# A node MLP run between edge groups: x added on VectorE, second product one chunk later

## The chip, the cores and the metric

The kernel runs on one NeuronCore of a Trainium2 chip. The metric is the device time of one execution in microseconds (us); lower is better. Three runs of the kernel before gave 4202.96 to 4210.07 us.

## What is computed

Two graph layers over 6,250 nodes and 200,000 edges, edges sorted by destination. The change touches the first:

```python
e = edge_attr @ W_edge + b_edge
msg = jax.nn.relu(x[src] + e)
agg = jax.ops.segment_sum(msg, dst, num_segments=x.shape[0])
h = (1.0 + eps) * x + agg
h = jax.nn.relu(h @ W1 + b1) @ W2 + b2
mean = jnp.mean(h, axis=0)
var = jnp.var(h, axis=0)
h = (h - mean) * jax.lax.rsqrt(var + BN_EPS) * gamma + beta
return jax.nn.relu(h)
```

A layer norm of x + h follows, then an attention layer and another layer norm. Everything is float32.

## The kernel before

**Groups.** Layer 0 walks over 196 groups of 1,024 edges. GpSimd (POOL) fetches a group's source rows with 8 indirect DMAs of 128 rows (`gather`, L377) into one of 4 slots of `rows`. TensorE (PE) multiplies the group's edge features in two halves (`edge_products`, L854, after a bias product L851) into banks 0 and 1 (half 0) or 2 and 3 (half 1). VectorE (DVE) adds each half into the rows (`add_edges`, L972), ScalarE (ACT) applies Relu (L952), and PE sums the messages into a window of 128 nodes with one-hot matrices (`sum_half`, L865), ACT copies the window (L956), PE transposes it (`turn_window`, L874) and DVE adds it into `acc` (`add_window`, L986). PE's body for group g holds the transposition of g-3, the second half of the sums of g-2, the first half of the products of g, the first half of the sums of g-1, and the second half of the products of g.

**What ties the engines.** POOL may start the gathers of group g when PE has finished the first products of group g-2:

```python
pool.wait_ge(half_done, 2 * (g - RING) + 5)
```

PE in its turn needs DVE's adds of the group before (`added`), and DVE needs the gathered rows (`rows_in`).

**Chunks.** The nodes are split into 14 chunks of 448. Since the edges are sorted, a chunk's sums are complete long before the last group. `rounds` runs four groups at a time and calls `finish_nodes(c, at)` on each engine after the round in which chunk c is complete (`at` is that round's last group). In this run 13 chunks (0 to 12) are finished in this way between rounds, 24 and 16 groups apart at first, 12 and 8 later and 4 between the last two; the last chunk (13) is finished after all groups by `last_nodes`. I call the 13 places boundaries.

**A boundary before.** PE makes three products of four matmuls each: x by (1+eps)W1 (`w1x`, L896) and the sums in `acc` by W1 (L901), which accumulate in banks 0 and 1; then, after ACT's Relu (L436), the second product by W2 (L909) into banks 2 and 3. Each matmul of 448 columns shows as two records, so a product is 8. PE then waits for ACT's copy with bias into `node_x` (L440) and only then goes on with the next group. DVE takes the statistics (`bn_stats`, L450) of the chunk before. SyncE (SP) loads x of a chunk into `x_in[0]` when PE has consumed the chunk before (`load_nodes`, L820). The end of layer 0 is the same three products for chunk 13, statistics, batch norm.

Of the kernel before, what the change touches and what calls it, by code (L numbers as in the profile page):

```python
# [22 lines left out]
ALU = mybir.AluOpType  # L23
# [6 lines left out]
P = 128  # L30
# [39 lines left out]
def build(nc, t):  # L70
    with ExitStack() as ctx:
# [3 lines left out]
        def sem(name):  # L75
            return ctx.enter_context(nc.semaphore(name))
# [179 lines left out]

        layer0, layer1 = Layer(0), Layer(1)
        half_done, added, bias_ready = sem("half_done"), sem("added"), sem("bias_ready")

        def two(name):  # L260
            return [sem(f"{name}{b}_") for b in range(2)]
# [555 lines left out]

        def single0_loads(sp):
            def load_nodes(c, at):
                sp.wait_ge(a_pe1, HALF * c)  # L820
                sp.sem_inc(passed, 1)
                sp.dma_start(x_in[0], t["x_t"][:, :, bass.ds(c * CHUNK, CHUNK)]).then_inc(a_in, 16)

            def body(i, u, g):
                if first_round(i):
                    return
                sp.wait_ge(layer0.rows_in[u], 16 * J * i)
                sp.dma_start(idx[:, u, :], t["src_idx"][g]).then_inc(layer0.idx_in[u], 16)
# [14 lines left out]
        def single0_matmuls(pe):  # L843
# [42 lines left out]
                    sum_half((u - 1) % RING, g - 1, 0, n < 3)  # L886
                edge_products(i, u, g, 1).then_inc(half_done, 1)

            def finish_nodes(c, at):
                pe.wait_ge(w1x_ready, 1)  # L890
                pe.wait_ge(a_in, 16 * c + 16)
                pe.wait_ge(a_act2, c)
                pe.wait_ge(added, 2 * at + 1)
                for m in range(HALF):
                    for k in range(HALF):
                        pe.matmul(banks[m][:, 0:CHUNK], w1x[:, k, m * P:(m + 1) * P], x_in[0][:, k, :],  # L896
                                  start=(k == 0), stop=False)
# [13 lines left out]
                last.then_inc(a_pe2, 1)  # L911
                pe.wait_ge(a_act2, c + 1)

            def finish_last(c, at):
                pe.wait_ge(w1x_ready, 1)
                pe.wait_ge(a_in, 16 * c + 16)
                pe.wait_ge(a_act2, c)
                for m in range(HALF):
                    for k in range(HALF):
                        pe.matmul(banks[m][:, 0:CHUNK], w1x[:, k, m * P:(m + 1) * P], x_in[0][:, k, :],  # L920
                                  start=(k == 0), stop=False)
                pe.wait_ge(layer0.group_done, GROUPS)
                for m in range(HALF):
                    for k in range(HALF):
                        last = pe.matmul(banks[m][:, 0:CHUNK], w1[:, k, m * P:(m + 1) * P],
                                         acc[:, k, bass.ds(c * CHUNK, CHUNK)], start=False, stop=(k == HALF - 1))
                    last.then_inc(a_pe1, 1)
                for m in range(HALF):
                    for k in range(HALF):
                        if m == 0:  # L930
                            pe.wait_ge(a_act1, 2 * c + k + 1)
                        last = pe.matmul(banks[2 + m][:, 0:CHUNK], w2[:, k, m * P:(m + 1) * P], x_in[1][:, k, :],
                                         start=(k == 0), stop=(k == HALF - 1))
                last.then_inc(a_pe2, 1)
# [13 lines left out]
        def single0_act(act):  # L948
            def relu(u, g, b):
                act.wait_ge(added, 2 * g + b + 1)  # L950
                half = rows[:, u, 4 * b:4 * b + 4, 0:D]
                act.activation(half, half, ACT.Relu).then_inc(layer0.msg_ready, 1)  # L952

            def copy_window(u, g, halves):
                act.wait_ge(half_done, halves)
                act.copy(agg_sb[:, 0:D], banks[4 + u % 2][:, 0:D]).then_inc(layer0.agg_copied, 1)  # L956

            def body(i, u, g):
                relu(u, g, 0)
# [3 lines left out]
            c0 = rounds(act, body, mlp_act(act, 0, 2))  # L963
            copy_window((GROUPS - 2) % RING, GROUPS - 2, 2 * GROUPS + 1)
            copy_window((GROUPS - 1) % RING, GROUPS - 1, 2 * GROUPS + 3)
            last_nodes(act, mlp_act(act, 0, 2), c0)

        def single0_vector(dve):
            def add_edges(i, u, g, b):
                dve.wait_ge(half_done, 2 * g + b + 1)  # L970
                half = rows[:, u, 4 * b:4 * b + 4, 0:D]
                dve.tensor_tensor(half, half, psum[:, 2 * b:2 * b + 2, :].rearrange("p b (j d) -> p (b j) d", j=2),  # L972
                                  ALU.add).then_inc(added, 1)

            def make_onehot(u, g):
                for j in range(J):
                    last = dve.tensor_scalar(onehot[:, u % 2, j, :], iota[:, :],  # L977
                                             dst_off[:, bass.ds(g, 1), j:j + 1].rearrange("p g j -> p (g j)"), None,
                                             ALU.is_equal)
                last.then_inc(layer0.onehot_ready, 1)  # L980

            def add_window(u, g, halves):
                base = dve.value_load(plan[0:1, 0, bass.ds(g, 1)], min_val=0, max_val=NODES)
                at = bass.ds(base, WIN)
                dve.wait_ge(half_done, halves)
                dve.tensor_tensor(acc[:, :, at], acc[:, :, at],  # L986
                                  banks[6 + u % 2][:, 0:HALF * WIN].rearrange("p (k n) -> p k n", k=HALF), ALU.add)
                dve.drain().then_inc(layer0.group_done, 1)

            def body(i, u, g):  # L990
                dve.wait_ge(layer0.rows_in[u], 16 * J * (i + 1))
# [5 lines left out]
            c0 = rounds(dve, body, mlp_dve(dve, 1))  # L997
# [185 lines left out]
        def _(pe):  # L1183
# [7 lines left out]
                single0_matmuls(pe)  # L1191
            with pe.Else():
                pass_matmuls(pe, layer0, 0)
            pe.wait_ge(a_act2, CHUNKS)

            def mean_over(x, out, done):
                for k in range(HALF):
# [49 lines left out]
        def _(act):  # L1247
# [6 lines left out]
                single0_act(act)  # L1254
            with act.Else():
                pass_act(act, layer0, 0)
            act.wait_ge(bn_var, 1)
            act.activation(bn_tmp[:, :], mv[:, :, 1], ACT.Sqrt, bias=bn_eps[:, :]).then_inc(bn_sqrt, 1)
            act.wait_ge(bn_ready, 1)
# [343 lines left out]
```

## Time and profile before

| | |
|---|---|
| median of three runs | 4208.57 us (4202.96 to 4210.07) |
| the profiled execution's own time | 4207.65 us |
| its span, first to last instruction | 4205.7 us |
| layer 0 (first gather to the last Relu'd node product) | about 3 to 2066 us of the span |
| mean granted TensorE clock | 0.879 |
| busy share over the span: PE, PE weight loads, DVE, ACT, POOL | 75%, 57%, 55%, 19%, 73% |

Times in rows are microseconds from the start of the span. PE is TensorE, PEld its weight loads, POOL GpSimd, SPq or ACTq an engine's queue. Brackets at the end of a timeline row give the engine's idle time before it and what released it. A granted clock of 1.00 is 2.4 GHz and 0.50 is 1.2 GHz.

### The profile page before, as it was taken

To read this page: it belongs to the slowest core of one execution; us is meant where nothing else is said; L and a number is where in the kernel's file an instruction comes from. 1 tells how busy PE (TensorE), PEld (TensorE's weight loads), DVE (VectorE), ACT (ScalarE), POOL (GpSimd) and SP (SyncE) were. 2 spreads that over 40 slices of the span, in tenths; PEclk is the share of its full clock that TensorE was granted. 3 is DMA by queue.
4 is the path that set the end of the run, shared out by engine and by line. 5 is a ranking of instruction groups with operands and counts; after the bars stand their busy time and mean duration, and the time that the engine had idled before them with its cause. 6 is when DMAs were issued, how large, how long until landed. Compare 5 with 4: busy or idle time off the path is not lost.

```text
span 4205.7 us, 55810 instructions
## 1 busy us (share of the span) xinstructions
PE 3147.9 (75%) x13605; PEld 2400.0 (57%) x13705; DVE 2322.7 (55%) x5665; ACT 798.6 (19%) x1490; POOL 3064.9 (73%) x3229
## 2 busy tenths in 40 slices
PE   7888788898888888889876666666666666666666
PEld 5666666676666666767554444444444444444544
DVE  5444444344444443434476666666666666766676
ACT  2222222222222222222240000010110111111112
POOL 7777777777777777767347777777777777777775
PEclk9999999999999999999897777877878778788777
DMA  5555555455545454545245555555555555555554
GB/s 186 154 157 155 155 158 157 151 158 153 154 149 166 152 153 148 168 140 163 74 128 157 160 157 156 161 160 160 162 156 165 161 161 164 160 165 161 160 169 122
DMA packets 321499, 651.40 MB, mean 155 GB/s; under 512 B 149711, under 2 KB 170425, under 8 KB 321465
## 3 DMA queue, kind: packets, MB, share of 16 engines
q0 software_dynamic: 150528, 414.45, 34.3%
q1 hardware_dynamic: 164448, 230.16, 17.5%
q10 hardware_dynamic: 6489, 6.40, 0.5%
q8 instruction: 12, 0.20, 0.0%
q14 instruction: 22, 0.18, 0.0%
HBM read 637.67 MB, written 13.08 MB: 155 GB/s over the span
## 4 chain that ended last, share of the span: by engine, by line
POOL 30%; PE 23%; issue 18%; DMA 12%; DVEq 7%; DVE 6%; ACT 2%; ACTq 1%; POOLq 1%; SPq 0%
POOL rows L377 30%; PE psum L865 7%; PE psum L854 7%; DMA rows<-z_tab,idx 6%; DMA rows<-in_x,idx 5%; DVEq L731 4%; DVE rows L972 2%; PE psum L851 1%; PE psum L584 1%; PE psum L874 1%; DVEq L727 1%; PE psum L909 1%; PE psum L896 1%; PE psum L1217 1%; PE psum L901 1%
## 5 line engine op out<-in xcount | busy, mean ns | idle before, releaser
L377 POOL DMA_INDIRECT rows<-in_x,idx x1568 | 1510.2, 963 | 531.8 <-issue 450.0
L377 POOL DMA_INDIRECT rows<-z_tab,idx x1568 | 1503.6, 959 | 482.5 <-issue 455.5
L972 DVE TENSOR_TENSOR rows<-rows,psum 128x1024 f32<-128x1024 f32 x392 | 478.5, 1221 | 1153.7 <-DMA rows<-in_x,idx 803.3
L584 PE MATMUL psum<-rows,onehot 128*128 128x260 f32 x3136 | 1059.5, 511 | 23.6 <-issue 23.3
L584 PEld LDWEIGHTS psum<-rows,onehot 128*128 128x128 f32 x3136 | 805.8, 263 | 208.8 <-issue 32.0
L854 PE MATMUL psum<-weights,edge_room 128*128 128x256 f32 x3136 | 816.7, 384 | 6.3 <-issue 1.5
L865 PE MATMUL psum<-rows,onehot 128*128 128x256 f32 x3136 | 776.9, 393 | 0.0
L854 PEld LDWEIGHTS psum<-weights,edge_room 128*128 128x128 f32 x3136 | 607.3, 194 | 161.1 <-issue 8.2
L952 ACT ACTIVATE rows<-rows 128x1024 f32<-128x1024 f32 x392 | 414.3, 1057 | 1491.7 <-DVE rows L972 1491.6
L865 PEld LDWEIGHTS psum<-rows,onehot 128*128 128x128 f32 x3136 | 602.3, 197 | 78.1
L801 DVE TENSOR_TENSOR rows<-rows,psum 128x1024 f32<-128x1024 f32 x392 | 460.7, 1216 | 77.9 <-ACT psum L673 77.9
L578 PE MATMUL psum<-ed_win,hot_t 128*128 128x12 bf16 x1576 | 72.6, 172 | 447.0 <-DVE hot_t L722 447.0
L670 ACT ACTIVATE rows<-expo 128x32 f32<-128x32 f32 x196 | 44.9, 229 | 1574.8 <-DVE expo L705 1567.1
L578 PEld LDWEIGHTS psum<-ed_win,hot_t 128*128 128x128 bf16 x1576 | 55.3, 101 | 503.7 <-DVE hot_t L722 252.2
L977 DVE TENSOR_SCALAR onehot<-iota,dst_off 128x128 f32<-128x128 f32 x1568 | 328.1, 296 | 0.0
L758 DVE TENSOR_TENSOR onehot<-dst_off,psum 128x1024 f32<-128x1024 f32 x196 | 239.3, 1221 | 85.1 <-issue 84.8
L398 PE MATMUL psum<-ident,agg_sb 128*128 128x128 f32 x392 | 82.0, 292 | 260.3 <-ACT agg_sb L639 260.3
L874 PE MATMUL psum<-ident,agg_sb 128*128 128x128 f32 x392 | 84.1, 297 | 250.6 <-ACT agg_sb L956 202.3
L851 PE MATMUL psum<-onehot 128*128 128x512 bf16 x685 | 264.1, 386 | 9.0 <-DVEq L1383 7.0
L697 DVE TENSOR_TENSOR score<-score,rows 128x32 f32<-128x32 f32 x196 | 38.1, 194 | 388.0 <-DMA rows<-z_tab,idx 382.9
L722 DVE TENSOR_SCALAR hot_t<-dst_t,node_at 128x256 bf16<-128x256 int32 x788 | 236.8, 362 | 0.1
L398 PEld LDWEIGHTS psum<-ident,agg_sb 128*128 128x128 f32 x392 | 39.9, 142 | 334.6 <-issue 334.6
(152 smaller groups left out, 1787.6 us busy)
## 6 DMA issues: line engine op xcount, KB each, us to landing
dst_t<-in_dst_jp SPq DMA_DIRECT2D x197, 512.0 KB
edge_room<-in_edge_t SPq DMA_DIRECT2D x196, 512.0 KB, 3.9
rows<-in_x,idx POOLq DMA_INDIRECT x1568
rows<-z_tab,idx POOLq DMA_INDIRECT x1568
dst_t<-in_x_t SPq DMA_DIRECT2D x28, 448.0 KB, 5.3
z_tab<-edge_room SPq DMA_DIRECT2D x14, 455.0 KB, 3.5
idx<-in_src_idx SPq DMA_DIRECT2D x392, 4.0 KB, 1.6
out<-onehot ACTq DMA_DIRECT2D x13, 448.0 KB, 3.4
```

The costliest lines, as they stand in the source:

```text
L377: nc.gpsimd.indirect_dma_start(rows[:, u, j, 0:width], None, table, bass.IndirectOffsetOnAxis(ap=idx[:, u, j:j + 1], axis=0)).then_inc(L.r ...
L584: last = pe.matmul(agg_ps[0:WIN, 0:width], onehot[:, hot, j, :], rows[:, u, j, 0:width], start=(j == 0), stop=(j == J - 1))
L722: last = dve.tensor_scalar(hot_t[:, part], dst_t[:, u % 2, part], node_at[:, bass.ds(g, 1)], None, ALU.is_equal)
L731: dve.drain().then_inc(L.group_done, 1)
L758: dve.tensor_tensor(onehot[:, hot, :, :], off.unsqueeze(2).to_broadcast([P, J, WIN]), iota_ps.unsqueeze(1).to_broadcast([P, J, WIN]), ALU. ...
L801: dve.tensor_tensor(z, z, w.unsqueeze(3).to_broadcast([P, J // 2, HEADS, HEAD_D]), ALU.mult).then_inc(L.msg_ready, 1)
L851: pe.matmul(bank[:, 0:2 * D], ones_bf[:, :], bias_rhs[:, :], start=True, stop=False)
L854: last = pe.matmul(bank[:, h * D:(h + 1) * D], edge_in[:, u, j * P:(j + 1) * P], w_edge[:, :], start=False, stop=(h == 1))
L865: last = pe.matmul(banks[4 + u % 2][:, 0:D], onehot[:, u % 2, j, :], rows[:, u, j, 0:D], start=(j == 0), stop=(j == J - 1))
L952: act.activation(half, half, ACT.Relu).then_inc(layer0.msg_ready, 1)
L972: dve.tensor_tensor(half, half, psum[:, 2 * b:2 * b + 2, :].rearrange("p b (j d) -> p (b j) d", j=2), ALU.add).then_inc(added, 1)
L977: last = dve.tensor_scalar(onehot[:, u % 2, j, :], iota[:, :], dst_off[:, bass.ds(g, 1), j:j + 1].rearrange("p g j -> p (g j)"), None, ALU ...
```

## The change

DVE adds (1+eps)x into `acc` for the chunk (one `scalar_tensor_tensor` over 128x896), counted by a new semaphore `a_sum`. PE's first product is then one product of `acc` by W1, into banks 2 and 3. The second product of chunk c is made at the boundary of chunk c+1, into banks 0 and 1, before the first product of chunk c+1; that of chunk 12 is made after the loop over all groups. ACT does its bias of chunk c-1 before the Relu of chunk c. DVE's statistics come two chunks later at a boundary, and those of the chunks left over stand ahead of the last `add_window`. SP's load of x waits for DVE's addition and no longer for PE. PE and ACT wait for the constants at the start. At the end of a boundary PE waits for both Relus of chunk c. `w1x` is still made, and no longer used in this path.

```diff
         def single0_loads(sp):
             def load_nodes(c, at):
-                sp.wait_ge(a_pe1, HALF * c)
+                sp.wait_ge(a_sum, c)
...
-            def finish_nodes(c, at):
-                pe.wait_ge(w1x_ready, 1)
-                pe.wait_ge(a_in, 16 * c + 16)
-                pe.wait_ge(a_act2, c)
-                pe.wait_ge(added, 2 * at + 1)
+            def first_product(c):
+                pe.wait_ge(a_sum, c + 1)
                 for m in range(HALF):
                     for k in range(HALF):
-                        pe.matmul(banks[m][:, 0:CHUNK], w1x[:, k, m * P:(m + 1) * P], x_in[0][:, k, :],
-                                  start=(k == 0), stop=False)
-                pe.wait_ge(layer0.group_done, at + 1 - LAG)
+                        last = pe.matmul(banks[2 + m][:, 0:CHUNK], w1[:, k, m * P:(m + 1) * P],
+                                         acc[:, k, bass.ds(c * CHUNK, CHUNK)], start=(k == 0), stop=(k == HALF - 1))
+                    last.then_inc(a_pe1, 1)
+
+            def second_product(c):
+                pe.wait_ge(a_act1, 2 * c + 2)
                 for m in range(HALF):
                     for k in range(HALF):
-                        last = pe.matmul(banks[m][:, 0:CHUNK], w1[:, k, m * P:(m + 1) * P],
-                                         acc[:, k, bass.ds(c * CHUNK, CHUNK)], start=False, stop=(k == HALF - 1))
-                    last.then_inc(a_pe1, 1)
-                pe.wait_ge(added, 2 * at + 2)
-                for m in range(HALF):
-                    for k in range(HALF):
-                        if m == 0:
-                            pe.wait_ge(a_act1, 2 * c + k + 1)
-                        last = pe.matmul(banks[2 + m][:, 0:CHUNK], w2[:, k, m * P:(m + 1) * P], x_in[1][:, k, :],
+                        last = pe.matmul(banks[m][:, 0:CHUNK], w2[:, k, m * P:(m + 1) * P], x_in[1][:, k, :],
                                          start=(k == 0), stop=(k == HALF - 1))
                 last.then_inc(a_pe2, 1)
+
+            def finish_nodes(c, at):
+                pe.wait_ge(added, 2 * at + 1)
+                with pe.If(c > 0):
+                    second_product(c - 1)
+                pe.wait_ge(added, 2 * at + 2)
+                first_product(c)
                 pe.wait_ge(a_act2, c + 1)
+                pe.wait_ge(a_act1, 2 * c + 2)
 
             def finish_last(c, at):
...
+                first_product(c)
+                pe.wait_ge(a_act2, c + 1)
+                second_product(c)
 
             pe.wait_ge(bias_ready, 1)
+            pe.wait_ge(const_in, 16 * WEIGHT_LOADS)
             c0 = rounds(pe, body, finish_nodes)
+            pe.wait_ge(added, 2 * GROUPS - 1)
+            with pe.If(c0 > 0):
+                second_product(c0 - 1)
...
+            def first_relu(c):
+                for k in range(HALF):
+                    act.wait_ge(a_pe1, 2 * c + k + 1)
+                    act.activation(x_in[1][:, k, :], banks[2 + k][:, 0:CHUNK], ACT.Relu,
+                                   bias=cols[:, 0, k:k + 1]).then_inc(a_act1, 1)
...
+            def finish_nodes(c, at):
+                with act.If(c > 0):
+                    act.reg_mov(before, c - 1)
+                    second_bias(act.snap(before, min_val=0, max_val=CHUNKS - 2))
+                first_relu(c)
...
+            def add_nodes(c):
+                chunk = acc[:, :, bass.ds(c * CHUNK, CHUNK)]
+                dve.wait_ge(a_in, 16 * c + 16)
+                dve.scalar_tensor_tensor(chunk, x_in[0], eps1[:, 0:1], chunk, ALU.mult, ALU.add).then_inc(a_sum, 1)
...
+            def finish_nodes(c, at):
+                add_nodes(c)
+                earlier_statistics(c, 2)
...
             add_window((GROUPS - 2) % RING, GROUPS - 2, 2 * GROUPS + 3)
+            earlier_statistics(c0, 2)
+            earlier_statistics(c0, 1)
             add_window((GROUPS - 1) % RING, GROUPS - 1, 2 * GROUPS + 4)
-            last_nodes(dve, mlp_dve(dve, 2), c0)
+            last_nodes(dve, finish_last, c0)
```

## Rows read from the trace of the kernel before

**Rows 1.** Groups of instructions, whole span: line, engine, operation, count, busy and mean ns
```profile
L377 POOL DMA_INDIRECT rows<-in_x,idx x1568 | 1510.2, 963 | 531.8 <-issue 450.0 <-PE psum L854 80.9 <-DMA idx<-in_src_idx 1.0
...
L436 ACT ACTIVATE dst_t<-psum,cols 128x448 f32<-128x448 f32 x28 | 17.7, 633 | 25.8 <-PE psum L901 19.7 <-PE psum L925 6.1
...
L1428 DVE TENSOR_TENSOR rows<-rows,edge_room 128x896 f32<-128x896 f32 x14 | 15.3, 1092 | 2.4 <-issue 0.5
```

**Rows 2.** Waits of POOL, 43 to 2045 us: total us, times, longest
```profile
POOL rows L377 <- issue: 440.8, 1409, 1.9
POOL rows L377 <- PE psum L854: 80.9, 128, 7.0
```

**Rows 3.** Timeline of POOL: gathers that start late, all behind boundaries
```profile
593.73 0.95 POOL L377 DMA_INDIRECT rows<-in_x,idx  x1 [1.67 <-PE psum L854]
...
841.23 0.95 POOL L377 DMA_INDIRECT rows<-in_x,idx  x1 [4.42 <-PE psum L854]
...
1006.28 0.95 POOL L377 DMA_INDIRECT rows<-in_x,idx  x1 [3.19 <-PE psum L854]
1009.10 0.96 POOL L377 DMA_INDIRECT rows<-in_x,idx  x1 [1.87 <-issue]
...
1679.07 0.95 POOL L377 DMA_INDIRECT rows<-in_x,idx  x1 [2.22 <-PE psum L854]
...
1974.96 0.95 POOL L377 DMA_INDIRECT rows<-in_x,idx  x1 [3.20 <-PE psum L854]
...
2022.23 0.95 POOL L377 DMA_INDIRECT rows<-in_x,idx  x1 [7.03 <-PE psum L854]
```

**Rows 4.** Chain in order of time at the third boundary: start, us, what
```profile
984.85 1.23 DVE rows L972
...
986.12 3.27 PE psum L896 x8
...
992.40 3.26 PE psum L909 x8
...
997.04 2.33 issue
999.37 0.59 PE psum L874 x2
```

**Rows 5.** Timeline of DVE at the same boundary
```profile
988.24 1.22 DVE L972 TENSOR_TENSOR rows<-rows,psum 128x1024 f32<-128x1024 f32 x1 [0.19 <-issue]
```

**Rows 6.** Windows behind two boundaries: last three numbers clock, DMA, GB/s
```profile
999.40:1006.30 6.90, 6.90 (x26) 5.63 (x27) 0.89 (x1) 0.00 (x0) 2.88 (x4) 0.75 0.26 76
588.50:593.70 5.20, 5.20 (x25) 4.45 (x26) 0.84 (x1) 0.00 (x0) 2.87 (x3) 1.00 0.34 101
```

**Rows 7.** Timeline of PE, last two boundaries
```profile
1968.05 0.44 PE L874 MATMUL psum<-ident,agg_sb 128*128 128x128 f32 x2 [3.72 <-issue]
...
2001.75 3.17 PE L896 MATMUL psum<-dst_t,w1x 128*128 128x448 f32 x8
...
2014.03 0.68 PE L874 MATMUL psum<-ident,agg_sb 128*128 128x128 f32 x2 [2.85 <-issue]
```

**Rows 8.** Timeline of the end of layer 0
```profile
2055.65 3.24 PE L920 MATMUL psum<-dst_t,w1x 128*128 128x448 f32 x8
2056.19 0.42 DVE L986 TENSOR_TENSOR acc<-acc,psum 128x256 f32 x1 [0.83 <-PE psum L874]
...
2058.73 3.17 PE L925 MATMUL psum<-acc,weights 128*128 128x448 f32 x8
```

**Rows 9.** Timeline of DVE and POOL near the start
```profile
17.14 1.79 DVE L1343 TENSOR_TENSOR dst_off<-node_x,first_f 128x1568 f32<-128x1568 int32 x1
...
18.07 1.69 POOL L377 DMA_INDIRECT rows<-in_x,idx  x1 [0.30 <-issue]
```

**Rows 10.** Timeline of DVE, start
```profile
25.76 5.39 DVE L1384 MEMSET acc<- 128x6400 f32 x1 [1.48 <-DMA hot_t<-in_att_dst]
...
32.36 1.22 DVE L972 TENSOR_TENSOR rows<-rows,psum 128x1024 f32<-128x1024 f32 x1 [0.62 <-PE psum L854]
```

More of the change, by code:

```diff
@@ L258, in build @@
         half_done, added, bias_ready = sem("half_done"), sem("added"), sem("bias_ready")
+        a_sum = sem("a_sum")
         def two(name):
@@ L910, in finish_nodes @@
                                          start=(k == 0), stop=(k == HALF - 1))
                 last.then_inc(a_pe2, 1)
+            def finish_nodes(c, at):
[4 more added lines that the diff above has]
+                first_product(c)
                 pe.wait_ge(a_act2, c + 1)
+                pe.wait_ge(a_act1, 2 * c + 2)
             def finish_last(c, at):
-                pe.wait_ge(w1x_ready, 1)
@@ L916, in finish_last @@
[L916 to L934, printed above, removed]
+                first_product(c)
+                pe.wait_ge(a_act2, c + 1)
+                second_product(c)
@@ L962, in body, with second_bias, finish_last @@
                 relu(u, g, 1)
-            c0 = rounds(act, body, mlp_act(act, 0, 2))
+            def first_relu(c):
[3 more added lines that the diff above has]
+                                   bias=cols[:, 0, k:k + 1]).then_inc(a_act1, 1)
+            before = act.alloc_register("chunk_before")
+            def second_bias(c):
+                act.wait_ge(a_pe2, c + 1)
+                for k in range(HALF):
+                    ins = act.activation(node_x[:, k, bass.ds(c * CHUNK, CHUNK)], banks[k][:, 0:CHUNK],
+                                         ACT.Identity, bias=cols[:, 1, k:k + 1])
+                ins.then_inc(a_act2, 1)
+            def finish_nodes(c, at):
[3 more added lines that the diff above has]
+                first_relu(c)
+            def finish_last(c, at):
+                first_relu(c)
+                second_bias(c)
+            act.wait_ge(const_in, 16 * WEIGHT_LOADS)
+            act.sem_inc(a_act2, 1)
+            c0 = rounds(act, body, finish_nodes)
+            with act.If(c0 > 0):
+                act.reg_mov(before, c0 - 1)
+                second_bias(act.snap(before, min_val=0, max_val=CHUNKS - 2))
             copy_window((GROUPS - 2) % RING, GROUPS - 2, 2 * GROUPS + 1)
             copy_window((GROUPS - 1) % RING, GROUPS - 1, 2 * GROUPS + 3)
-            last_nodes(act, mlp_act(act, 0, 2), c0)
+            last_nodes(act, finish_last, c0)
         def single0_vector(dve):
@@ L996, in body, with statistics, earlier_statistics, finish_last @@
                 add_edges(i, u, g, 1)
-            c0 = rounds(dve, body, mlp_dve(dve, 1))
+            prev = dve.alloc_register("prev_chunk_single")
+            def add_nodes(c):
+                chunk = acc[:, :, bass.ds(c * CHUNK, CHUNK)]
+                dve.wait_ge(a_in, 16 * c + 16)
+                dve.scalar_tensor_tensor(chunk, x_in[0], eps1[:, 0:1], chunk, ALU.mult, ALU.add).then_inc(a_sum, 1)
+            def statistics(c, n):
+                for k in range(HALF):
+                    dve.bn_stats(stats[:, k, bass.ds(c, 1), :].rearrange("p a s -> p (a s)"),
+                                 node_x[:, k, bass.ds(c * CHUNK, n)])
+            def earlier_statistics(c, back):
+                with dve.If(c > back - 1):
+                    dve.wait_ge(a_act2, c + 2 - back)
+                    dve.sem_inc(passed, 1)
+                    dve.reg_mov(prev, c - back)
+                    statistics(dve.snap(prev, min_val=0, max_val=CHUNKS - 2), CHUNK)
+            def finish_nodes(c, at):
+                add_nodes(c)
+                earlier_statistics(c, 2)
+            def finish_last(c, at):
+                add_nodes(c)
+                dve.wait_ge(a_act2, c + 2)
+                statistics(c, TAIL if isinstance(c, int) else CHUNK)
+            c0 = rounds(dve, body, finish_nodes)
             add_window((GROUPS - 3) % RING, GROUPS - 3, 2 * GROUPS + 1)
             add_window((GROUPS - 2) % RING, GROUPS - 2, 2 * GROUPS + 3)
+            earlier_statistics(c0, 2)
+            earlier_statistics(c0, 1)
             add_window((GROUPS - 1) % RING, GROUPS - 1, 2 * GROUPS + 4)
-            last_nodes(dve, mlp_dve(dve, 2), c0)
+            last_nodes(dve, finish_last, c0)
         def nodes(i, b):
@@ L1193, in _ @@
                 pass_matmuls(pe, layer0, 0)
-            pe.wait_ge(a_act2, CHUNKS)
+            pe.wait_ge(a_act2, CHUNKS + 1)
             def mean_over(x, out, done):
@@ L1256, in _ @@
                 pass_act(act, layer0, 0)
+                act.sem_inc(a_act2, 1)
             act.wait_ge(bn_var, 1)
```

## The prediction

> **What bounds the kernel now.** I read the groups of instructions first. POOL's gathers are the largest: 0.96 us each, and with the 0.30 us that normally lies between two (the bracket of the gather in [rows 9]) a group of eight takes 10.1 us [rows 1]. The change touches layer 0 alone, so the question is when POOL does not keep that pace there. The waits of POOL say it: 128 times the gather came behind a product of PE, 80.9 us in all [rows 2]. At 0.30 us each, 38.4 of these are its ordinary gap; 42.5 are real. The timeline of POOL shows where: one late gather behind each of the 13 boundaries, 1.4 us over the ordinary gap at the first, about 2.9 at six, about 4 at three (the row at 841 us stands for them), 1.9 at one, 2.9 at the twelfth, 6.7 at the last [rows 3]; 0.6 of the 42.5 lies at the start, before any boundary. Behind seven of them the second gather is late too, by 1.57 us, as at 1009.10 [rows 3]. What POOL loses to boundaries is therefore 41.9 + 7 x 1.57 = 52.9 us. That is the stake. Between boundaries PE waits for rows, and what PE does there costs nothing.
>
> The chain in order of time at one boundary gives the mechanism [rows 4]. Call the start of DVE's addition of half 0 of the last group t0 (984.85). PE starts the x product at t0+1.27, three products follow one another, two ACT copies end at 997.04, and then come 2.33 us that no wait explains: PE's loop turn and its reads of the next limits. PE resumes at t0+14.52. The late gather started at 1006.28, 2.89 us late [rows 3], so POOL was ready at 1003.39, t0+18.54, and from resuming to that gather PE needed 6.91 us. With the clock at 1.00 that stretch is 5.2 us; here it had 0.75 on average [rows 6].
>
> **Removed from PE's path.** The x product is gone, and the second product moves ahead of the first, where it needs nothing that is new. I lay the new boundary out in the same frame.
>
> - PE: second product of c-1 from t0+1.27. The branch before it is not in the trace; below it cannot be under 0, above I take the whole 2.33 us of the loop turn [rows 4], and I use 0.3, since the loop turn holds several branches and loads. It ends at 1.27+0.3+3.26 = t0+4.85.
> - DVE: its addition of half 1 starts at 988.24, t0+3.39, takes 1.22 us [rows 5], and the next instruction starts about 0.06 before its end, at t0+4.55. The new addition over 128x896 is priced by the 1.09 us of the tensor-tensor of that size with both inputs in SBUF [rows 1]; a form with one more operand may cost up to 1.3. I take 1.1: sums ready at t0+5.65. This, and not the second product, releases PE, so 0.8 us of branch are covered.
> - PE: first product, from a standing start 3.27 us [rows 4]: t0+8.92. ACT's second Relu, 0.63 us and some 0.1 for two semaphores [rows 1]: t0+9.65. The loop turn 2.33: PE resumes at t0+12.0, 2.5 us earlier than before.
> - ACT: its bias of c-1 (two copies, 1.2 us) falls after its Relu of half 1, between t0+5.7 and t0+7; the first Relu is ready for it only at t0+7.4. Covered, and late by 0.7 us if the second product comes 1.5 us late.
> - DVE's statistics, SP's load of x and the constants: the statistics stand where DVE waits for PE afterwards. The load waits for t0+5.65 of the boundary before instead of the end of PE's second of three products; it is a whole boundary early. The constants have landed when DVE's memset starts at 25.76, while DVE's first addition starts only at 32.36 behind other work [rows 10]; PE's start slips by at most 1.5 us under that. All nothing.
>
> **The clock.** The idle time before PE resumes was 3.72 us at the boundary before the last and 2.85 at the last [rows 7]; it becomes 12.0-8.9 = 3.1. At the last one the clock fell all the same, and at the first, after a longer idle time, it stayed at 1.00 [rows 6]. I count on no gain here and leave the stretch of 6.91 us (5.2 to 8.2) as each boundary had it.
>
> **What remains of the eleven boundaries before 1954 us.** They cost 41.9-2.9-6.7 = 32.3 in first gathers and six times 1.57 = 9.4 in second ones: 41.7. With PE 2.5 earlier the three of about 4 keep 1.6, 1.2 and 1.6 = 4.4; the six of 2.9 keep 0.4; the two short ones nothing.
>
> **What the new addition does to POOL.** DVE's instruction with two SBUF inputs ran from 17.14 to 18.93; the gather that started in it at 18.07 took 1.69 us instead of 0.96 [rows 9]: it was held 0.73, that is the 0.86 that DVE still had, less 0.13. At our boundary the gathers start every 1.26 us back from 1003.39, one of them at 989.5, t0+4.65, just inside the new addition (4.55 to 5.65): held by about 0.87. Other boundaries lie a little differently (nothing to 1.0); I take 0.75. POOL is the bound, so this counts, except where it waits for PE anyway. So eight boundaries lose 0.75 each (6.0, the 0.4 is inside) and three lose 4.4: 10.4. The eleven give back 41.7-10.4 = 31.3 us.
>
> A page of the Trainium skill, SBUF — State Buffer, section Who interferes with whom, says that a VectorE instruction with two SBUF inputs contends only with GpSimd reads, and infers that a tensor-tensor does not stall descriptor generation. By that inference the hold would be 0, the eleven would lose 6.8 and the sum below would be 3.6 us better; [rows 9] speak against it.
>
> **The last two boundaries and the end.** From 1968.05 on PE is the bound: it goes through four groups and reaches the last boundary at 2001.75 without idle time [rows 7]. There the order before took 12.28 us. New: 0.3 + 3.0 (second product, back to back) + 3.27 + 0.73 for the Relu + 1.5 loop turn (the 2.85 of idle time less ACT's last copies) = 8.8, 3.5 less. With the 2.5 of the twelfth boundary PE is 6.0 us earlier. After the groups it has one second product more, 3.26+0.3, on its path. For chunk 13 the x product started at 2055.65 and the next at 2058.73 [rows 8]. New: the last addition into `acc` ends at 2056.6, the new addition at 2057.8, the first product at 2061.1, and the second starts after both Relus at 2061.8, where it was 2061.9. So the end costs 3.4. The three together give 6.0-3.4 = 2.6 us.
>
> **Sum.** 31.3+2.6 = 33.9 us from the profiled execution's 4207.65: 4173.7. The median of the runs is 0.9 higher: **4174.5 us**.
>
> **Rivals.**
> - *Nothing is held and the clock stays up* (more gain). For it: the first boundary kept 1.00 [rows 6], and the new idle time is shorter than at eleven of them. All 41.7 come back, plus 6.0-3.4, plus up to 2.8 twice for clock on PE's last stretch: 44 to 50 us, 4158 to 4164; the missing hold alone gives 4171, inside my own case. Chance 0.17. The inference of the Trainium skill's page SBUF — State Buffer, named above, is the first half of it.
> - *POOL still stalls* (less gain). The branch costs 2.33 and the new addition 1.3: PE resumes 1.5 to 1.7 later than I laid out, first gathers gain only about 0.9 each, the second gathers stay late: eleven boundaries give some 11 us, the end nothing: 8 to 20 us, 4188 to 4200. Against it: each branch inside the 2.33 can only be a part of it. Chance 0.14.
> - *Slower.* One mechanism: the new conditional blocks make PE's queue fetch code out of order on entering and on leaving, 2.33 us each, 4.7 in all. 0.8 is covered, so PE resumes 3.9-2.5 = 1.4 later than before, 13 x 1.4 = 18 us and 2 at the end: 4228. It decides from 3.4 us per boundary on. For it is only that 2.33 us of the loop turn are unexplained. Chance 0.05. The Trainium skill, Runtime: NRT & Kernel Launch, section Instruction fetch mechanics, says that a taken branch to code outside the fetched pages stalls for a fetch; no row here shows one at a boundary by itself.
> - *The change moves nothing*: POOL's late gathers have another cause than PE's return, say the transfers. Against it, their size follows PE's: 5.2 us after resuming with the clock at 1.00, 6.9 with it at 0.75 [rows 6]. Chance 0.03.
>
> **Chances and range.** My case, 26 to 42 us of gain, has 0.61. Within 0.2% (8.4 us, about what a measurement of this kernel can tell from no change) I put 0.03, above it 0.05, below 0.92. The likeliest case alone is 4166 to 4183. The range of 8 in 10 takes in most of the first rival and the upper part of the second: 4158 to 4191.
>
> **What would show it.** The three products at a boundary become two, with the second first; the span from t0 to PE's next transposition is 12.0 instead of 14.5. POOL's waits behind L854 fall from 80.9 towards 45, the 1.87 rows go mostly; one gather of 1.7 us stands beside each new addition. The first transposition after a boundary has about 3.1 us of idle time before it. Between boundaries a group still takes 10.1 us, and layer 1 is unchanged. The prediction is wrong if PE's resume moves by less than 1 us (branch), if the gathers at boundaries are held for more than 1 us, or if POOL's late gathers keep their size while PE comes earlier.

## The result and the profile after

The changed kernel takes 4180.19 us (median of 4 runs, 4174.65 to 4182.70) beside 4205.76 us (4 runs, 4200.05 to 4210.07): 0.9936 of the time before, 95% interval 0.9921 to 0.9952, 25.6 us less. Two more samples, each beside its own runs of the kernel before, gave 0.9932 (0.9920 to 0.9944) and 0.9934 (0.9921 to 0.9948). The profiled execution took 4182.70 us with a span of 4180.9, 24.8 less than the span of before.

The groups of instructions, whole span (columns as in [rows 1]):

```profile
L378 POOL DMA_INDIRECT rows<-in_x,idx x1568 | 1522.9, 971 | 484.9 <-issue 448.6 <-PE psum L855 35.3 <-DMA idx<-in_src_idx 1.0
...
L1020 DVE SCALAR_TENSOR_TENSOR acc<-dst_t,eps,acc 128x896 f32 (+1 forms) x14 | 16.0, 1146 | 0.3 <-issue 0.3
```

POOL's idle time before the gathers of layer 0 fell from 531.8 to 484.9, and its busy time rose from 1510.2 to 1522.9 [rows 1]: the change gives and takes on the same engine. The addition takes 1.15 us. The waits of POOL, 43 to 2110 us:

```profile
POOL rows L378 <- issue: 439.5, 1428, 1.9
POOL rows L378 <- PE psum L855: 35.3, 109, 1.5
```

Beyond the ordinary 0.30 us, these waits for PE come to 35.3 - 109 x 0.30 = 2.6 us, where they were 42.5 [rows 2]. Some late gathers now stand under "issue" as well. All gathers that start late behind a boundary, added up gather by gather, lose 5.9 us, where they lost 52.9. The chain at the third boundary says how, start, length, what; t0 is 983.79 here:

```profile
988.24 1.16 DVE acc L1020
989.40 0.24 issue
989.63 3.28 PE psum L894 x8
992.91 0.02 issue
992.94 0.64 ACT dst_t L954
993.58 2.37 issue
995.96 0.68 PE psum L875 x2
```

DVE's addition starts at t0+4.45 and releases PE's first product; one Relu and the loop turn follow, and PE resumes at t0+12.17; before it was 14.52 [rows 4]. The timeline of the same stretch, DVE, POOL and PE:

```profile
983.79 1.22 DVE L990 TENSOR_TENSOR rows<-rows,psum 128x1024 f32<-128x1024 f32 x1 [5.52 <-DMA rows<-in_x,idx]
...
984.70 0.96 POOL L378 DMA_INDIRECT rows<-in_x,idx  x1 [0.30 <-issue]
...
985.30 3.27 PE L902 MATMUL psum<-dst_t,weights 128*128 128x448 f32 x8 [0.72 <-DVE rows L990]
...
988.24 1.14 DVE L1020 SCALAR_TENSOR_TENSOR acc<-dst_t,eps,acc 128x896 f32 x1
...
988.59 1.63 POOL L378 DMA_INDIRECT rows<-in_x,idx  x1 [0.30 <-issue]
...
989.30 1.15 DVE L1024 BATCH_NORM_STATS2 stats<-node_x  x2
989.32 1.14 ACT L962 ACTIVATE node_x<-psum,cols 128x448 f32 x2
...
995.96 0.68 PE L875 MATMUL psum<-ident,agg_sb 128*128 128x128 f32 x2 [3.05 <-issue]
996.43 3.62 PE L866 MATMUL psum<-rows,onehot 128*128 128x256 f32 x8
...
1004.10 0.95 POOL L378 DMA_INDIRECT rows<-in_x,idx  x1 [1.25 <-PE psum L855]
...
1006.92 0.95 POOL L378 DMA_INDIRECT rows<-in_x,idx  x1 [1.87 <-issue]
```

The deferred second product runs from t0+1.5 to t0+4.8, in the time in which PE would wait for DVE. The gather that starts inside the addition takes 1.63 us; the one at 984.70, which starts inside DVE's addition into `rows` (one input in SBUF, one in PSUM), takes 0.96. The late gather is 0.95 us late, not 2.89 [rows 3], and the second one still 1.57; here the clock fell after the boundary (3.62 us for eight records instead of 1.89).

The end of layer 0, timeline:

```profile
2023.75 0.44 PE L875 MATMUL psum<-ident,agg_sb 128*128 128x128 f32 x2 [0.46 <-ACT agg_sb L944]
2024.50 2.21 DVE L1024 BATCH_NORM_STATS2 stats<-node_x  x4 [0.66 <-issue]
2026.62 0.40 DVE L1004 TENSOR_TENSOR acc<-acc,psum 128x256 f32 x1
2027.36 1.15 DVE L1020 SCALAR_TENSOR_TENSOR acc<-dst_t,eps,acc 128x896 f32<-128x896 f32 x1 [0.33 <-issue]
2028.56 5.33 PE L894 MATMUL psum<-acc,weights 128*128 128x448 f32 x8 [4.38 <-DVE acc L1020]
```

Before, the last transposition started at 2055.27 and the last addition into `acc` 0.9 us later, at 2056.19 [rows 8]. Here the addition stands behind four statistics and comes 2.9 us after the transposition's start, and PE then runs the first product with the clock down, 5.33 us for eight records. From the start of the last gather to the end of the last bias copy it is 30.5 us; before it was 23.5. Up to the last transposition it is 2.6 us more, behind it 4.3.

How far the profiled execution is ahead of the one before, place by place:

| place | before | after | ahead |
|---|---|---|---|
| t0 of the first boundary | 573.70 | 575.44 | -1.7 |
| t0 of the twelfth | 1953.52 | 1929.63 | 23.9 |
| PE resumes after the last | 2014.03 | 1982.48 | 31.6 |
| last gather starts | 2042.81 | 2008.66 | 34.2 |
| last bias copy ends | 2066.34 | 2039.15 | 27.2 |
| span | 4205.7 | 4180.9 | 24.8 |

### The profile page after: what moved, and what is told of

It is laid out like the page before. It is cut to its first block, busy times and chain, and to the rows that moved or that the text cites. A ratio compares the mean times of both kernels' runs of the same rounds, so it can differ in the third digit from the quotient of the medians.

```text
span 4180.9 us, 55635 instructions
## 1 busy us (share of the span) xinstructions
PE 3078.4 (74%) x13493; PEld 2355.7 (56%) x13593; DVE 2339.0 (56%) x5679; ACT 797.3 (19%) x1490; POOL 3078.8 (74%) x3229
## 3 DMA queue, kind: packets, MB, share of 16 engines
q1 hardware_dynamic: 164448, 230.16, 17.8%
## 4 chain that ended last, share of the span: by engine, by line
POOL 31%; PE 19%; issue 19%; DMA 12%; DVEq 8%; DVE 7%; ACT 2%; ACTq 1%; POOLq 1%; SPq 0%
POOL rows L378 31%; DMA rows<-z_tab,idx 7%; PE psum L866 6%; PE psum L855 6%; DMA rows<-in_x,idx 5%; DVEq L732 5%; DVE rows L990 2%; DVEq L728 1%; PE psum L852 1%; PE psum L474 1%; PE psum L1265 1%; PE psum L875 1%; PE psum L1246 1%; PE psum L894 1%; DVE rows L802 1%
## 5 line engine op out<-in xcount | busy, mean ns | idle before, releaser
L378 POOL DMA_INDIRECT rows<-in_x,idx x1568 | 1522.9, 971 | 484.9 <-issue 448.6
L585 PE MATMUL psum<-rows,onehot 128*128 128x260 f32 x3136 | 1024.8, 498 | 23.7 <-issue 23.6
L585 PEld LDWEIGHTS psum<-rows,onehot 128*128 128x128 f32 x3136 | 781.5, 255 | 198.4 <-issue 32.0
L866 PEld LDWEIGHTS psum<-rows,onehot 128*128 128x128 f32 x3136 | 600.4, 197 | 78.2
L995 DVE TENSOR_SCALAR onehot<-iota,dst_off 128x128 f32<-128x128 f32 x1568 | 329.9, 298 | 0.0
```

Of the source, the lines that this page charges most:

```text
L378: nc.gpsimd.indirect_dma_start(rows[:, u, j, 0:width], None, table, bass.IndirectOffsetOnAxis(ap=idx[:, u, j:j + 1], axis=0)).then_inc(L.r ...
L585: last = pe.matmul(agg_ps[0:WIN, 0:width], onehot[:, hot, j, :], rows[:, u, j, 0:width], start=(j == 0), stop=(j == J - 1))
L866: last = pe.matmul(banks[4 + u % 2][:, 0:D], onehot[:, u % 2, j, :], rows[:, u, j, 0:D], start=(j == 0), stop=(j == J - 1))
```

## The experiments

The times are medians of 5 to 12 runs; each ratio is to the kernel before in the same job. PE's return is the median over the boundaries of its profile, measured from t0.

| kernel | us | ratio (95%) | PE resumes | last gather to last bias copy |
|---|---|---|---|---|
| changed, 2nd sample | 4177.59 | 0.9932 (0.9920 to 0.9944) | t0+12.2 | 30.2 |
| addition only | 4251.10 | 1.0111 (1.0097 to 1.0124) | 17.8 | 23.2 |
| deferral only | 4197.80 | 0.9977 (0.9969 to 0.9986) | 14.0 | 27.4 |
| one SBUF input | 4175.98 | 0.9928 (0.9916 to 0.9940) | 12.2 | 30.8 |
| addition, wait filled | 4226.12 | 1.0048 (1.0035 to 1.0062) | 16.0 | 24.8 |
| late statistics | 4182.03 | 0.9936 (0.9922 to 0.9949) | 12.2 | 25.8 |
| split addition | 4176.52 | 0.9931 (0.9918 to 0.9945) | 11.7 | 30.0 |
| split, late statistics | 4175.44 | 0.9926 (0.9912 to 0.9939) | 11.7 | 26.4 |
| changed, 3rd sample | 4181.84 | 0.9934 (0.9921 to 0.9948) | 12.2 | 30.5 |
| split, late statistics, 2nd | 4174.24 | 0.9917 (0.9904 to 0.9931) | 11.7 | 27.9 |
| and second product moved | 4169.30 | 0.9910 (0.9896 to 0.9923) | 11.7 | 24.2 |
| the same, addition whole | 4173.49 | 0.9916 (0.9902 to 0.9929) | 12.2 | 24.2 |

**The changed kernel again**, unedited, in two jobs.

> The changed kernel once more, as the measure for the other runs on this chip. Both theories: 24 to 27 us under the kernel before, PE resumes 12.2 us after DVE's first addition of the boundary (t0), 12 gathers of 1.6 to 1.9 us, two to five late gathers behind the first boundaries.

> The changed kernel once more, on the chip of the next three, since differences of 2 to 10 us are at stake: 24 to 29 us under the kernel before.

Measured 30.1 and 26.5 us under the kernel before, the first more than expected. PE's return was the same in all three profiles; the late gathers varied (5.9, 9.2 and 11.2 us in all), and so did the number of boundaries behind which the clock fell: 4, 7 and 8 of 13. In the profile of the kernel before it fell behind 11.

**The addition alone.** Against the kernel before:

```diff
                 pe.wait_ge(a_act2, c)
                 pe.wait_ge(added, 2 * at + 1)
-                for m in range(HALF):
-                    for k in range(HALF):
-                        pe.matmul(banks[m][:, 0:CHUNK], w1x[:, k, m * P:(m + 1) * P], x_in[0][:, k, :],
-                                  start=(k == 0), stop=False)
-                pe.wait_ge(layer0.group_done, at + 1 - LAG)
+                pe.wait_ge(a_sum, c + 1)
                 for m in range(HALF):
...
-            c0 = rounds(dve, body, mlp_dve(dve, 1))
+            c0 = rounds(dve, body, added_first(mlp_dve(dve, 1)))
```

`added_first` puts `add_nodes(c)` of the changed kernel ahead of DVE's statistics; the second product stays in banks 2 and 3.

> One part alone: DVE adds (1+eps)x and PE's first product has four matmuls, but the second product stays at its own chunk and the statistics where they were. My theory: the gain needs both parts. The sums are ready at t0+5.65, first product to 8.9, second product to 12.2, ACT's two copies to 13.6, PE's loop turn to t0+16.0, that is 1.5 us later than the kernel before (14.5), because PE stands idle while DVE works. POOL's late gathers grow by 1.5 us each and 12 gathers are held: 15 to 25 us slower than the kernel before. The rival, that the gain is the 3.0 us of matmuls saved per boundary, expects about the gain of the whole change or more, 25 to 38 us faster than before.

Measured 43.4 us slower: the direction right, the size twice what I expected. POOL's late gathers come to 81.4 us instead of 52.9, and 12 gathers are held, 8.9 us in all. Timeline of PE and ACT at a boundary with t0 at 1124.64:

```profile
1130.49 4.74 PE L896 MATMUL psum<-acc,weights 128*128 x8 [5.05 <-DVE acc L990]
1133.76 0.63 ACT L437 ACTIVATE dst_t<-psum,cols 128x448 f32<-128x448 f32 x1 [3.49 <-PE psum L896]
1135.06 3.41 PE L904 MATMUL psum<-dst_t,weights 128*128 128x448 f32 x8
```

PE waited 5.05 us for DVE and then took 4.74 us for a product that takes 3.27 elsewhere: the clock fell inside it (1.00 from 1124.6 to 1130, 0.79 on average from 1130 to 1138). PE resumed at t0+17.6 here. The same product took 4.7 to 6.3 us at 12 of the 13 boundaries. Four matmuls fewer, and slower, because the work taken away had been lying under DVE's additions.

**The deferral alone.** Against the changed kernel:

```diff
-            def first_product(c):
-                pe.wait_ge(a_sum, c + 1)
+            def first_product(c, done):
+                pe.wait_ge(w1x_ready, 1)
+                pe.wait_ge(a_in, 16 * c + 16)
+                for m in range(HALF):
+                    for k in range(HALF):
+                        pe.matmul(banks[2 + m][:, 0:CHUNK], w1x[:, k, m * P:(m + 1) * P], x_in[0][:, k, :],
+                                  start=(k == 0), stop=False)
+                pe.wait_ge(layer0.group_done, done)
                 for m in range(HALF):
...
-                add_nodes(c)
                 earlier_statistics(c, 2)
```

> The other part alone: the x product stays on PE (w1x), the second product of a chunk comes at the next boundary, DVE adds nothing; the statistics are two chunks late as in the change. My theory: second product to t0+4.9, x product to 7.9, product of the sums to 10.9, Relu and loop turn to t0+13.9, 0.6 us earlier than the kernel before and 1.8 later than the change; no gather is held; the late gathers stay at 2 us each, less 1.7 where the clock no longer falls. At the end of layer 0 some 5 us more than before. In all 5 to 20 us faster than before, so less than the change. A rival, that the deferral is the whole gain and the addition on DVE adds nothing, expects 25 us or more, as in the change.

Measured 9.9 us faster than the kernel before, as expected. The chain at the boundary with t0 at 1235.82:

```profile
1235.82 1.23 DVE rows L995
1237.05 0.27 issue
1237.32 3.27 PE psum L907 x8
1240.59 3.17 PE psum L894 x8
1243.77 3.02 PE psum L899 x8
1246.79 0.02 issue
1246.81 0.64 ACT dst_t L959
1247.45 2.37 issue
1249.83 0.43 PE psum L874 x2
```

Three products in a row, only one Relu and the loop turn behind them: t0+14.0, as worked out. No gather is held, POOL's late gathers sum to 34.2 us. So the parts do not add: +43 and -10 apart, -30 together in the same job.

**One SBUF input.** The output lacks (1+eps)x.

```diff
-    dve.scalar_tensor_tensor(chunk, x_in[0], eps1[:, 0:1], chunk, ALU.mult, ALU.add).then_inc(a_sum, 1)
+    dve.bn_stats(onehot[:, 2, 3, 0:6], acc[:, 0, bass.ds(c * CHUNK, CHUNK)])
+    dve.bn_stats(onehot[:, 2, 3, 6:12], acc[:, 1, bass.ds(c * CHUNK, CHUNK)]).then_inc(a_sum, 1)
```

> The changed kernel with DVE's addition of x replaced by two bn_stats over the chunk's sums (448 columns each, one SBUF input) into a spare tile, so (1+eps)x is left out of the result; DVE works as long (1.15 us), PE waits for it in the same way. My theory: the gathers of 1.63 us at the boundaries are held by the addition's second SBUF input, so they fall back to 0.96 and the last gather starts 7 to 9 us earlier than in the changed kernel; time 6 to 9 us less than the changed kernel. Rival, that gathers are long there for another reason (transfers, PE's products, any DVE work): the long gathers stay and the time is that of the changed kernel.

The mechanism was right, its worth was not. Of the 12 gathers of 1.62 us or more at the boundaries none is left, and PE resumes at the same t0+12.2. `bn_stats` also writes far less than the addition, so this run alone does not tell the second input from the writing. The trace of the changed kernel does: 389 gathers start inside DVE's addition into `rows`, which writes 128x1024 with one input in SBUF and one in PSUM, and none takes more than 0.97 us; all 12 that start inside the addition of x take 1.62 to 1.83.

The time is only 1.6 us less, inside the spread. The last gather starts 3.7 to 4.0 us earlier than in the first two profiles of the changed kernel and 7.1 earlier than in the third, not 7 to 9 throughout: POOL's late gathers sum to 14.7 us instead of 5.9 to 11.2. At some boundaries POOL now waits for PE in the time in which it was held before. The clock also fell behind more of them, 9 of 13, and the run does not part the two.

**The wait filled.** The addition alone, with a product that is thrown away in PE's wait. SyncE's load of x waits for PE again.

```diff
                 pe.wait_ge(added, 2 * at + 1)
+                pe.wait_ge(w1x_ready, 1)
+                pe.wait_ge(a_in, 16 * c + 16)
+                for m in range(HALF):
+                    for k in range(HALF):
+                        pe.matmul(banks[m][:, 0:CHUNK], w1x[:, k, m * P:(m + 1) * P], x_in[0][:, k, :],
+                                  start=(k == 0), stop=(k == HALF - 1))
                 pe.wait_ge(a_sum, c + 1)
```

> DVE's addition alone, as in add_only, but PE fills its wait for it: the x product of the kernel before (w1x, eight records) runs from t0+1.3 to 4.5 into banks 0 and 1 and is overwritten by the first product. It is work without use. My theory: in add_only PE stood idle 5 us before the first product, the clock fell inside it and PE resumed at t0+17.6 where the order of instructions alone gives 16.1; filled, the first product takes 3.3 again at every boundary, PE resumes at t0+16.1, and the time falls by 12 to 25 us against add_only, though PE does more. Rival, that add_only is slow for the longer order alone: PE resumes no earlier and the time is that of add_only.

Timeline of PE at the boundary with t0 at 1117.1:

```profile
1118.42 3.27 PE L897 MATMUL psum<-dst_t,w1x 128*128 128x448 f32 x8 [0.60 <-DVE rows L967]
1122.80 3.27 PE L902 MATMUL psum<-acc,weights 128*128 x8 [1.11 <-DVE acc L996]
1125.91 3.41 PE L910 MATMUL psum<-dst_t,weights 128*128 128x448 f32 x8
```

With eight records more of work PE resumes 1.7 us earlier (t0+16.0) and the kernel is 25 us faster than the addition alone (the two were measured in different jobs, each beside the kernel before). The deferred product does the same in the changed kernel with work that is needed. Behind a wait of 5.05 us the product took 4.74 us, behind one of 1.11 us 3.27, and so at all 13 boundaries here: 3.17 or 3.27. The Trainium skill, TensorE: Matmul & The Clock Gate, section Why this matters for your kernels, advises against long idle gaps between bursts of matmuls. The trace agrees, by these numbers.

**Late statistics.**

```diff
     add_window((GROUPS - 2) % RING, GROUPS - 2, 2 * GROUPS + 3)
-    earlier_statistics(c0, 2)
-    earlier_statistics(c0, 1)
     add_window((GROUPS - 1) % RING, GROUPS - 1, 2 * GROUPS + 4)
...
                 add_nodes(c)
-                dve.wait_ge(a_act2, c + 2)
+                if isinstance(c, int):
+                    earlier_statistics(c, 2)
+                    earlier_statistics(c, 1)
+                    dve.wait_ge(a_act2, c + 2)
...
```

> The changed kernel with the statistics of chunks 11 and 12 moved behind the last addition into acc and behind the addition of x for chunk 13. My theory: at the end of layer 0 they stand on the path from the last transposition to the last sums, 2.3 us; PE's idle time before chunk 13's first product falls from 4.4 to about 2 and the product may keep its clock (3.3 instead of 5.3). Last gather to the last bias copy takes 2 to 4.5 us less; time 2 to 4.5 us less than the changed kernel. Rival, that they fill a wait that is there anyway: no difference at the end.

The end took 25.8 us instead of 30.2 to 30.5, as expected; the time, 4182.03, shows nothing of it, where I expected 2 to 4.5 us less. In the profiled execution the gathers had fallen behind before the first boundary (t0 577.6, in all the others 573.7 to 575.6), but this does not explain the median of the five runs. The changed kernel was not in this job. What 4.5 us are worth cannot be read from one such sample.

**Split addition.**

```diff
-                chunk = acc[:, :, bass.ds(c * CHUNK, CHUNK)]
-                dve.scalar_tensor_tensor(chunk, x_in[0], eps1[:, 0:1], chunk, ALU.mult, ALU.add).then_inc(a_sum, 1)
+                for k in range(HALF):
+                    chunk = acc[:, k, bass.ds(c * CHUNK, CHUNK)]
+                    dve.scalar_tensor_tensor(chunk, x_in[0][:, k, :], eps1[:, 0:1], chunk,
+                                             ALU.mult, ALU.add).then_inc(a_sum, 1)
...
+                        if m == 0:
+                            pe.wait_ge(a_sum, 2 * c + k + 1)
```

> The changed kernel with DVE's addition in two instructions of 448 columns, one per half of the features, each counted by itself; PE starts the first product with half 0. My theory: DVE takes 0.15 us more, PE starts 0.5 us earlier and resumes at t0+11.7 instead of 12.2; a gather is held only by the part that is running, 0 to 0.45 us instead of 0.7 to 0.85. The late gathers left (6 to 9 us) fall by half: 3 to 8 us less than the changed kernel. Rival, that the hold is one of the whole addition however it is cut: gathers of 1.6 us stay.

Timelines of DVE and of POOL at one boundary:

```profile
989.02 1.27 DVE L1022 SCALAR_TENSOR_TENSOR acc<-dst_t,eps,acc 128x448 f32 x2
```

```profile
989.21 1.32 POOL L378 DMA_INDIRECT rows<-in_x,idx  x1 [0.30 <-issue]
```

The hold is 0.34 to 0.41 us at six boundaries and about 0.2 at six others, instead of 0.67 to 0.87 at 12, and PE resumes at t0+11.7: both parts as expected. The time did not follow (4176.52, where I expected 3 to 8 us less than the changed kernel). In this execution the clock fell behind 12 of 13 boundaries and late gathers came to 18.5 us.

**Both, and the second product moved.**

```diff
-    pe.wait_ge(added, 2 * GROUPS - 1)
-    with pe.If(c0 > 0):
-        second_product(c0 - 1)
     turn_window(u(GROUPS - 3), GROUPS - 3, False)
...
     turn_window(u(GROUPS - 1), GROUPS - 1, False).then_inc(half_done, 1)
     pe.wait_ge(added, 2 * GROUPS)
+    with pe.If(c0 > 0):
+        second_product(c0 - 1)
```

ACT's bias copy of chunk 12 moves with it, behind its last two window copies. The diff is against the kernel with the split and the late statistics.

> Both changes together. Both act at different places, so the sum of the two: 5 to 12 us less than the changed kernel, 0.8% to 1.0% under the kernel before.

> The kernel with the split addition and the late statistics once more, beside the changed kernel: if the single results were no chance, 2 to 6 us less than the changed kernel; if they were, no difference.

> The split addition, the late statistics, and the second product of chunk 12 moved behind the last transposition, where PE waits for the last sums and the addition of x for chunk 13. My theory: 3.2 us of product leave the path and fill a wait of about 2 us, and the first product of chunk 13 keeps its clock: from the last gather to the last bias copy 22 to 24 us instead of 26.4, and 4 to 9 us less than the changed kernel in all. Rival, that the product only moves along the same path: 26 us stay.

> The same without the split: the late statistics and the moved product with the addition in one instruction. It tells the end from the split: from the last gather to the last bias copy 22 to 25 us, long gathers of 1.63 us at the boundaries, time 4 to 8 us less than the changed kernel if the split gives nothing, and 1 to 3 more than the one with the split if it does.

The chain at the end of the kernel with all three:

```profile
2013.82 0.44 PE psum L875 x2
2014.26 3.06 PE psum L903 x8
2017.32 3.02 PE psum L895 x8
2020.34 0.02 issue
2020.36 0.64 ACT dst_t L954
2021.01 0.14 issue
2021.14 3.26 PE psum L903 x8
```

PE goes from the last transposition through chunk 12's second product straight into chunk 13's first, which takes 3.0 us instead of 5.3. This kernel takes 4169.30 us, 39.1 less than the one before and 12.5 less than the changed kernel in the same job, more than I expected; its slowest run (4171.77) is below the fastest of that one (4177.39). Without the split it is 4173.49, 8.4 less than the changed kernel, and here too no run overlaps (slowest 4176.72): the late statistics and the moved product together are worth something in time. The 4.2 us between these two, for the split, have overlapping intervals, so they are likely and not shown.

Split and late statistics without the move gave 4175.44 and 4174.24. The first is 1.1 us under the split alone in its job, and the changed kernel was not in it; the second is 7.6 us under the changed kernel beside it, again without overlap (slowest 4175.34) and more than the 2 to 6 expected. Their ends took 26.4 and 27.9 us. That difference is the clock's: behind the same wait of 1.98 us chunk 13's first product took 3.27 us in one and 4.74 in the other.

## Why the prediction came out as it did

Forecast 4174.5 us and a gain of 33.9; measured 4180.19 and 25.6, in the range (4158 to 4191) and inside the likeliest case's own (4166 to 4183). As a gain it is just under the 26 to 42 of that case, because a fourth run of the kernel before put its median 2.8 us lower. The mechanism held: POOL's late gathers were the stake, and PE's earlier return took them away. Over the kernels measured here they follow PE's return: 81.4 us in all at t0+17.8, 56.9 at 16.0, 52.9 at 14.6 (before), 34.2 at 14.0, and 5.9 to 14.7 at 12.2. Further down they do not: in the four kernels with the split addition, at 11.7, they are 7.3 to 18.5.

The terms of the sum, forecast and as this profile has them: the eleven boundaries 31.3 and 23.9, the last two 6.0 and 7.7, the end -3.4 and -7.0, layer 1 nothing and -2.4. A further 2.6 us came between PE's last return and the last gather, where the clock now stayed at 1.00. Together that is 24.8. The largest shortfall is that of the eleven boundaries, 7.4; the end has 3.6.

- *PE resumes at t0+12.0*: 12.17. Addition from t0+4.45 (4.55), 1.15 us (1.1), branch 0.24 (0.3), product 3.28 (3.27), loop turn 2.37 (2.33). At the first boundary it was t0+13.9 (14.0 and 12.2 in the other two profiles): chunk 0 has no second product before it, so PE's wait for DVE is not filled (3.5, 3.7 and 3.4 us), and its first product took 4.96 us twice and 3.27 once. I had not seen this.
- *A gather held 0.75 us per boundary*: 0.67 to 0.87 at 12 of 13. Each was held for what the addition still had to run, less 0.13 us, as I had read it from [rows 9] (0.80 left, held 0.67; 1.00 left, held 0.87). In the second profile it was 11 of 13: at one boundary the gather started 0.01 us after the addition and took 0.96. The run with one SBUF input and the gathers inside DVE's other additions show that the second SBUF input is the cause. Of the two readings that the prediction weighed, [rows 9] held: a gather is held by a two-input instruction, 0.67 to 0.87 us. The page SBUF — State Buffer of the Trainium skill (Who interferes with whom) infers no stall of descriptor generation from such an instruction, and the trace is against it for these gathers. Whether the gather's descriptors are held or its reading of the offsets in `idx`, which lies in SBUF, the trace does not tell.
- *The clock: no gain counted on*. It fell behind 4 to 8 boundaries instead of 11, so part of the first rival came true. That the shorter idle time (3.05 us instead of 3.7) did this is not shown: the kernel before has one profile here, and other kernels with 3.05 us had 5, 7, 9 and 11.
- *The eleven boundaries give 31.3*: the twelfth t0 came 23.9 earlier. Of the 41.7 lost before, 13.8 stayed (7.9 in holds, 5.9 in late gathers; I had 10.4), and 4.0 went elsewhere: 1.7 before the first boundary, the rest spread over ordinary gathers. This part moves from one execution to the next: the first t0 lay at 573.7 to 577.6 over all the kernels, which do nearly the same until then, and in the two other profiles of the changed kernel an ordinary gather took 0.956 us, as before, where it takes 0.958 here. Yet from the first t0 to the twelfth the three profiles come out alike, 25.6, 25.2 and 25.0 us shorter than before. One profile cannot charge the 4.0 to the change.
- *The last two boundaries give 6.0*: from the twelfth t0 to PE's last return it was 31.6 - 23.9 = 7.7. The clock stayed at 1.00 behind both; before it had fallen behind both.
- *The end costs 3.4*: this term failed. It cost 7.0 (30.5 against 23.5). The second product more cost 2.6 up to the last transposition, where I had 3.6; behind it I had no cost, and 4.3 were lost. I took the late statistics as lying "where DVE waits for PE afterwards". At a boundary they do; at the end they stand ahead of the last `add_window`, DVE reaches them only after the one before it, and 2.3 us fall on the path. With them PE's idle time grew to 4.38 us and the clock fell in the next product, 2.1 us more. Moving them brought the end to 25.8, moving the second product to 24.2.
- *Layer 1 unchanged*: it took 2.4 us more of the span in this execution, and 1.7 and 1.1 less in the two other profiles of the changed kernel. No instruction of it was changed, and it differs that much between executions.
- *Slower by fetches, no change*: nothing of either. The branch costs 0.24 us.
- *Small readings*: 1.27+0.3+3.26 is 4.83, not 4.85; the second product of chunk 13 started at 2061.74 before, not 2061.9; and the 0.6 us of late gather at the start is put down to "issue", so it is not in the 42.5. None of them moves the forecast by more than 0.2 us.

Not settled: why a second gather is late by 1.57 us behind some late ones and not behind others, what decides whether the clock falls behind a boundary, and what makes the gathers' pace drift between executions.

## What to carry to other kernels

Work that looks removable may be lying under somebody else's work. With the x product gone from PE, DVE adding x and nothing in its place, the kernel was 43 us slower; a useless product in that place gave 25 of them back; the gain came from putting other needed work there. When an operation moves to another engine, ask what that engine's new instruction holds up and whether the receiver of its result now stands idle. At a pipeline's end redo the layout by hand: a step that is free in every round (statistics, a deferred product) can stand on the path in the last one.

## What was not expected of the hardware

- A PE wait of 5.05 us ahead of a product cost 1.5 us inside it (4.74 against 3.27), and filling the wait with a useless product made the kernel 25 us faster.
- The clock behind boundaries that are alike falls at some and not at others, and the idle time before PE's return does not decide it: with 3.7 us it fell behind 11, 8 and 10 of 13 (before, addition only, wait filled); with 3.05 us behind 4, 7 and 8 (changed), 5, 7, 9 and 11; with about 3.15 us, in the four with the split addition, behind 9, 10, 10 and 12.
- Taking a hold off the bounding engine need not shorten the kernel by its length: with one SBUF input the holds were gone (8.6 us in the first profile of the changed kernel), late gathers grew by 3.5 to 8.8 us, and the time was 1.6 us less, inside the spread.
- A one-input instruction of DVE holds a gather too, by little: gathers that start inside the TENSOR_SCALAR of 128x128 f32 (L977 before, L995 after) take 1.02 us in the median and up to 1.08, others 0.96.
